# Scatters of the sorted rows tied one by one to the products of the expert stage

## What is computed

```python
x = x + tanh(g_xattn) * attention(layernorm(x), ctx)
xf = layernorm(x)
for j in range(2):                                  # two layers
    gate = xf @ router_W[j] + router_b[j]
    _, ids = top_k(gate + gate_bias[j], 2)          # two of six experts for each token
    weights = softmax(where(selected, gate, -inf))
    h = xf @ exp_Wup + exp_bup                      # for every expert e
    h = silu(h @ exp_Wg + exp_bg) * h
    combined = sum_e weights * (h @ exp_Wdown + exp_bdown)
    s = xf @ share_Wup + share_bup                  # two shared experts, for all tokens
    s = silu(s @ share_Wg + share_bg) * s
    y = xf + combined + (s @ share_Wdown + share_bdown).sum()
    xf = y * rsqrt(mean(y * y) + eps) * norm_w[j]
x = x + tanh(g_ffn) * xf
```

## Time and profile before

| | us |
|---|---|
| median of 3 runs (2814.58 to 2819.35) | 2816.75 |
| the profiled execution | 2810.69 |
| its span | 2808.6 |
| PE busy in it | 2489.5 (89%) |
| DVE busy | 1931.8 (69%) |
| ACT busy | 1576.7 (56%) |
| POOL busy | 478.8 (17%) |
| the 128 scatters (L966), POOL busy | 124.8 |
| the 128 gathers (L1700), POOL busy | 126.0 |

### The profile page before, as it was taken

One profiled execution on the slowest core, in us unless ns is written; L12 is line 12 of the kernel. 1 busy time (PEld: TensorE's weight loads), 2 busy tenths in 40 slices (PEclk: granted clock), 3 DMA queues, 4 the chain that ended last, 5 costly groups with the idle time before them and its releaser, 6 DMA issues. The chain is left out here.

```text
span 2808.6 us, 55075 instructions
## 1 busy us (share of the span) xinstructions
PE 2489.5 (89%) x20166; PEld 1507.6 (54%) x20166; DVE 1931.8 (69%) x3187; ACT 1576.7 (56%) x3345; POOL 478.8 (17%) x541
## 2 busy tenths in 40 slices
PE   7886999999999999999999998767599968969896
PEld 6773444444444444444444444666487857857675
DVE  8776888888888888888888882544234534634546
ACT  4440777777777777777777776322144423423432
POOL 2002000101010100000010102222303141340413
PEclk9996999999999999999999998768799989989998
DMA  7999757565665647475655623311234312321433
GB/s 267 400 359 237 96 81 104 77 90 75 91 83 85 88 71 104 70 105 67 92 82 85 81 40 90 129 63 57 75 92 120 92 68 61 110 90 35 147 98 98
DMA packets 164962, 305.70 MB, mean 109 GB/s; under 512 B 45607, under 2 KB 112334, under 8 KB 156366
## 3 DMA queue, kind: packets, MB, share of 16 engines
q1 hardware_dynamic: 151358, 265.56, 45.4%
q0 software_dynamic: 12288, 33.57, 3.8%
q10 hardware_dynamic: 1072, 3.23, 0.5%
HBM read 165.13 MB, written 127.68 MB: 104 GB/s over the span
## 5 line engine op out<-in xcount | busy, mean ns | idle before, releaser
L804 ACT ACTIVATE at_P<-at_ST 128x512 f32<-128x512 f32 (+4 forms) x2176 | 1095.9, 559 | 371.8 <-PE at_ST L847 349.5
L755 DVE TENSOR_REDUCE f_part<-at_R 128x2 f32<-128x804 f32 x1024 | 976.0, 994 | 121.1 <-PE at_R L835 117.1
L862 PE MATMUL at_OP<-at_P,at_V 128*32 128x256 f32 x8192 | 641.4, 385 | 16.0 <-ACT at_O L812 12.9
L847 PE MATMUL at_ST<-at_Q,at_K 64*128 64x512 f32 (+4 forms) x1428 | 343.9, 455 | 3.5 <-ACT at_P L804 3.5
L862 PEld LDWEIGHTS at_OP<-at_P,at_V 128*32 128x32 f32 x8192 | 163.1, 108 | 264.0 <-ACT at_P L804 186.7
L835 PE MATMUL at_R<-at_K,at_Q 64*128 64x402 f32 x1344 | 271.0, 392 | 5.1 <-DVE f_part L755 5.1
L738 POOL TENSOR_SCALAR_AFFINE_SELECT at_P<-at_P 128x512 f32<-128x512 f32 x128 | 81.6, 637 | 1088.8 <-ACT at_P L804 1088.8
L847 PEld LDWEIGHTS at_ST<-at_Q,at_K 64*128 64x128 f32 (+1 forms) x1428 | 141.7, 180 | 218.5 <-ACT at_P L804 203.6
L752 DVE TENSOR_REDUCE f_mx<-at_R 128x2 f32<-128x256 f32 (+3 forms) x256 | 209.9, 821 | 42.7 <-PE at_R L828 40.7
L1757 DVE TENSOR_TENSOR ex_ab<-ex_bank,ex_sg 128x256 f32<-128x256 f32 x148 | 62.8, 424 | 239.8 <-ACT ex_sg L1840 182.1
L1700 POOL DMA_INDIRECT ex_gb<-expert_rows,c_IDX x128 | 126.0, 984 | 430.3 <-DMA expert_rows<-ex_rb 314.1
(11 more groups left out here) (240 smaller groups left out, 4242.6 us busy)
## 6 DMA issues: line engine op xcount, KB each, us to landing
at_K<-k_parts SPq DMA_DIRECT2D x126, 264.1 KB, 9.1
k_parts<-pj_kpart SPq DMA_DIRECT2D x32, 800.5 KB, 9.5
ex_xb<-sorted SPq DMA_DIRECT2D x148, 128.0 KB
expert_rows<-ex_rb SPq DMA_DIRECT2D x148, 128.0 KB
v_items<-pj_vbuf SPq DMA_DIRECT2D x32, 544.0 KB, 9.5
q_parts<-pj_qpart SPq DMA_DIRECT2D x32, 512.0 KB, 11.0
at_Q<-q_parts SPq DMA_DIRECT2D x252, 64.0 KB, 9.8
f_K<-k_parts SPq DMA_DIRECT2D x60, 264.1 KB, 9.5
```

Source lines behind the costliest of these rows:

```text
L755: dve.tensor_reduce(part[:, :, p, q, c], buf[:, :, 0:XC], AX.X, ALU.max).then_inc(s_drain, 1)
L804: act.activation(Pt[(NKT * n + s) % NP][0:rows, h, c0:T], ST[(NST * n + s * G + h) % NB][0:rows, c0:T], ACT.Exp, scale=SCALE).then_inc(s_e ...
L847: pe.matmul(ST[t % NB][0:rows, c0:T], K[n % NU][half, p, keys], Q[n % NU][half, kind, p, c0:T], start=True, stop=True).then_inc(s_st, 1)
L862: ins = pe.matmul(OP[32 * h:32 * h + 2 * D, at], V[n % 2][0:rows, key_tile(s), h, :], Pt[(NKT * n + s) % NP][0:rows, h, at], start=s in (0 ...
```

## The change

`scatter` issues one DMA instead of two; the list holds 32 `SC` events for a round instead of 16 (in `stage_mix` the two are issued in a row as before). Each `SC` of `stage_experts` now waits, on GpSimd, for the last up product (`U` or `UP`) that stands ahead of it in the list; the table `pace` is made from the list. The places in the list are new too: the second 16 DMAs of round 0, which stood in a row at the head of the stage, are spread at every third event of the first shared stage; those of round 1 stand one at each of blocks 0 to 31; those of rounds 2 and 3 stand one behind each event of their shared stages.

```diff
-    def scatter(self, pool, r, t, XS, XR):
+    def scatter(self, pool, r, t, j, XS, XR):
 
         h = r % 2
-        if t == 0:
+        if t == 0 and j == 0:
             pool.wait_ge(self.s_gate, self.gate(r, self.NRO + 10))
-        for j in range(2):
-            pool.indirect_dma_start(XS[h], bass.IndirectOffsetOnAxis(ap=self.IDX[h][:, j, t:t + 1], axis=0),
-                                    XR[:, h * self.HT + t, :], None).then_inc(self.s_sc[h][t // QT], 16)
+        pool.indirect_dma_start(XS[h], bass.IndirectOffsetOnAxis(ap=self.IDX[h][:, j, t:t + 1], axis=0),
+                                XR[:, h * self.HT + t, :], None).then_inc(self.s_sc[h][t // QT], 16)
...
-        events += [("SC", 0, t) for t in range(HT // 2, HT)]
-        events += mixed(shared_events(0), ev + R.place(1), 1)
+        shared = mixed(shared_events(0), ev + R.place(1), 1)
+        events += mixed(shared, [("SC", 0, t, j) for t in range(HT // 2, HT) for j in range(2)], 3)
         for t in range(HT):
-            at(2 * t, 3, ("SC", 1, t))
+            for j in range(2):
+                at(2 * t + j, 3, ("SC", 1, t, j))
...
-            at(k1, 0, *shared[:first], *mixed(shared[first:], [("SC", NHF + r, t) for t in range(HT)], 3))
+            rows = [("SC", NHF + r, t, j) for t in range(HT) for j in range(2)]
+            at(k1, 0, *shared[:first], *mixed(shared[first:], rows, len(shared[first:]) // len(rows)))
...
+        pace, taken = {}, 0
+        for e in events:
+            if e in use:
+                taken = use[e] + 1
+            elif e[0] == "SC" and taken:
+                pace[e] = taken
...
                     if e[0] == "SC":
-                        R.scatter(pool, e[1], e[2], XS, XR)
+                        if e in pace:
+                            pool.wait_ge(s_a, pace[e])
+                        R.scatter(pool, *e[1:], XS, XR)
```

More of the change, by code:

```diff
@@ L1208, in _ @@
                     elif e[0] == "SC":
-                        R.scatter(pool, e[1], e[2], XS, XR)
+                        for j in range(2):
+                            R.scatter(pool, e[1], e[2], j, XS, XR)
             @block.vector
```

## The result

| | before | after |
|---|---|---|
| median, us | 2816.79 (2814.58 to 2819.35, 4 runs) | 2745.11 (2740.31 to 2748.24, 4 runs) |
| the profiled execution | 2810.69 | 2748.24 |
| its span | 2808.6 | 2746.2 |

The ratio of the medians is 0.9746, with a 95% interval of 0.9731 to 0.9761: the change takes 2.5% off, 71.7 us by the medians and 62.4 us by the two profiled executions. The forecast was 2760 us. The two differences disagree because the profiled execution of before lies 6.1 us under its median and that of after 3.1 us above its own; 62.4 + 6.1 + 3.1 = 71.6.

What follows compares the result with a forecast made beforehand. Expert blocks were taken as TensorE-bound, shared stages as held up by GpSimd's runs of scatters. 34 + 28 - 5 = 57 us off the 2816.75 us median gave 2760 us; forecast 2745 to 2775 (0.50), wider range 2730 to 2796.

Steps and rivals of the forecast that it cites:

- The cause: Shared stages: PE, ACT and DVE are held up while GpSimd issues scatter behind scatter; mechanism not shown by the trace.
- The rival that said otherwise: Shared stages: scatters are not the cause, something else in the same place stalls them; 2817 us, chance 0.04.
- First shared stage, forecast 34 us: First shared stage: losses of 30.3 and 6.4 us go, sixteen remaining scatters cost 2.4; gain 34 us.
- Second and third shared stage, forecast 14 us each: Rounds 2 and 3's shared stages: about 12 us of 26 lost remains, gain 14 us each, bounds 0 and 26.
- The walk: Rounds 2 and 3: GpSimd falls silent after eleven scatters, P3 comes 9 to 10 us late, later groups cost 3 us.
- behave like the gathers with pauses: Rounds 2 and 3, scatter groups after P3: act like paced gathers, not the run of 32; given 3 us.
- Blocks of round 0, forecast a loss of 5 us: Expert blocks 0 to 31: round 1's 32 scatters, one per block, cost 5 us; upper bound 26.
- The term's rate of 0.15 us each: Blocks of round 0: price per scatter, from 26 GpSimd instructions, mostly gathers, beside which PE idled 3.9 us.
- The rival that made the change slower: Blocks 0 to 31: every scatter costs a hold-up of its own, 87 us for 32; 2842 us, chance 0.06.
- Loads, forecast nothing: SP's load of a round's first block: scatters finish early enough, cost nothing; otherwise a few us each round.
- Neither sign of being wrong: DVE idle over 10 us released by "remote" in first shared stage, or PE below 19 of 20 us in round 0's blocks.

Runs made afterwards that it cites:

- e4: Changed kernel with rounds 2 and 3's scatters replaced by 32 small GpSimd power operations, nothing scattered there: 2719.0 us (1 run).
- e1: Changed kernel with the new product waits dropped in rounds 2 and 3, places in the list kept: 2771.03 us, 0.9864 of before.
- e3: Changed kernel with rounds 2 and 3's tiles sent by 32 plain DMAs from SP's queue, none from GpSimd: 2715.14 us (1 run).
- e10: Changed kernel without waits in rounds 2 and 3, GpSimd issuing 32 plain DMAs instead of indirect ones: 2721.2 us, before 2812.97 on that chip.
- e11: Changed kernel without waits in rounds 2 and 3, each scatter there moving only a quarter of each row: 2780.16 us (1 run).
- e12: Changed kernel without waits in rounds 2 and 3, eight small power operations after every twelfth scatter: 2731.07 us, before 2807.77 on that chip.
- e2: Changed kernel, waits kept, rounds 2 and 3's 32 scatters spread over products P0 to P13 instead of P0 to P9: 2718.89 us, 0.9688 of before.

## Why the prediction held, point by point

**The cause.** That the scatters are what stops PE, ACT and DVE held: e4 takes them away and P0 to P9 falls to 32.3 us, e1 brings them back unpaced and it is 58.5. The rival that said otherwise is out. The sentence of the Trainium skill on DMAs and engines, which it leaned on (SBUF — State Buffer, section "SBUF: two separate sides"), agrees with the transfers themselves: e3 and e10 move the same bytes beside the same products and slow nothing. With a row of indirect DMAs it doesn't agree: e1 and e11 lose 26 us and more in a stage, and there the measurement decides.

**First shared stage, forecast 34 us.** It went from 111.2 to 73.1, 38.1 us. The working had 36.7 for the loss of before, which was 1.4 too little (P0 to P9 went from 47.0 to 39.0 us, 8.0, where it had counted 6.4), and 2.4 for the sixteen scatters that stay, which was too much: 73.1 us is also what the stage takes on chip 13, so at 1 to 3 behind a product they cost nothing. The stage began 2.9 us later in the profiled execution of after; over all traces its P0 lies between 1908.0 and 1914.1 us, so that is how executions differ, and not the change.

**Second and third shared stage, forecast 14 us each.** P0 to P9 took 44.6 us where "about 44" was said, a gain of 14.0 and 13.7. The stages as a whole gained 17.4 and 13.9; the 3.4 us more of the second lie outside P0 to P9, where the change does nothing. The sum was right and its parts were not, so that it came out so close is luck. The walk expected the one big hold-up after P2, with P3 19 us behind P0, and 3 us for all later groups. P3 came 11.8 us behind P0 (2225.18 to 2237.01), against 9.3 in e3: 2.5 us lost. The first real hold-up fell on P4, which came 19.7 us behind P0 where e3 has 12.1, and the second on P9: 11.5 us from P8 to P9 (2258.26 to 2269.77) where 4.9 would do. Of the 12.3 us lost, nearly 10 were lost behind P3.

The step that failed is the sentence that the later groups "behave like the gathers with pauses". The table leaves them no pause. P4 to P8 release 16 scatters, 16 x 1.27 = 20.3 us of GpSimd's time, and from P4 to P9 the undisturbed products of e3 take 20.2 us; my estimate from e3's product times and 1.27 us a scatter is one run of all 32. The 16 in a row of the trace are these. When the engines come free after a hold-up, the held products also come through close together (P4 at 2244.89, P5 at 2246.85) and their releases stack up, but a run of 16 would stand there without that. What was right is that the wait is a brake: GpSimd fell silent after 13 scatters, and DVE ran again 2.4 us after the last of them ended (2241.55 + 0.96 to 2244.89). The loss of about 12 us of 26 came out by two middling hold-ups instead of one.

**Blocks of round 0, forecast a loss of 5 us.** Measured 2.2 (103.0 to 105.2). Even that is hardly the scatters' price as hold-ups: on chip 13, where nothing is held up, the same stretch with the same 32 scatters takes 104.1 to 105.6 us. The term's rate of 0.15 us each was taken from a stretch that has DVE's additions and eight gathers in a row; a single scatter per block has room of 2.88 us and costs no more than 0.07 us. The rival that made the change slower needed 1.9.

**Loads, forecast nothing.** Held: block 37 came 2.88 us behind block 36, and the first blocks of the later rounds also keep their period.

**What no step spoke of.** The stretches of gathers after UP36 and UP72 took 2.6 us more each, and the end 3.4 us less. The change moves nothing there. Over e1 to e4 and e10 to e12, which are alike there, the same stretches lie between 125.4 and 128.7, and 126.2 and 132.1 us, so most of it is the spread between executions, though 129.1 is 0.4 above the first range. In the first of these stretches the added time is PE's own: 745 matmuls are busy for 120.44 us in place of 117.87, at a mean granted clock of 0.95 in place of 0.97.

**The sum.** 57 us forecast, 62.4 in the profiled executions: +4.1 from the first stage, +3.3 from the other two, +2.8 from the blocks, -2.9 and -1.9 from the start and the rest. Neither sign of being wrong showed: no idle time of DVE in the first shared stage is released by "remote", and PE was busy 104.17 of 106 us in the blocks. The median of after, 2745.1, sits inside the forecast's own 2745 to 2775 only by its edge; 9.2 of the 14.9 us between it and 2760 is where the two profiled executions lie in their ranges.

## What to carry to other kernels

When several engines stop together beside a row of indirect DMAs of GpSimd, and the trace names no releaser, look at the length of the row, not at the DMA share, and spread them so that only a few stand together, or use plain DMAs where the addresses allow it. A wait for a product makes a pause only if the scatters that a product releases take less time than the product: multiply them out before you build the table (16 scatters of 1.27 us against 20.2 us of products left no pause here, and e2, with slack, took 34.5 us where the change took 44.6). Before a gain of this kind is believed for good, run before and after on more than one chip.
